# Another issue order on all engines in a windowed-attention, convolution and MLP block

## What is computed

```python
xw = windows(x)                            # 7x7 windows: 64 per image, 49 tokens, 96 channels
xn = layernorm(xw) * ln_g + ln_b
q, k, v = (xn @ qkv_w.T + qkv_b)           # 12 heads of 8
attn = softmax((q * SCALE) @ k.T + bias[REL_IDX])
out = attn @ v
seq = x + window_reverse(out @ proj_w.T + proj_b)
conv = depthwise_conv3x3(seq)              # 9 taps per channel, zero padding
seq2 = batchnorm(conv)                     # mean, variance, gain and shift are given
h = gelu(seq2 @ w1.T + b1)                 # 384 hidden
y = seq2 + (h @ w2.T + b2)
```

## Time and profile before

| | us |
|---|---|
| median of 3 runs | 3174.46 (3173.98 to 3175.64) |
| the profiled execution | 3164.1 |
| its span | 3162.3 |
| TensorE busy | 3029.4 (96%) |
| VectorE busy | 2888.8 (91%) |
| ScalarE busy | 2768.5 (88%) |
| GpSimd busy | 1956.6 (62%) |
| granted TensorE clock, mean | 0.993 of full |

### The profile page before, as it was taken

The page is one execution under the profiler, slowest core; times in us unless marked ns, Lnnn a source line. Parts: engine busy times, 40 slices in busy tenths (PEclk is TensorE's granted clock), DMA queues, the critical chain, the costliest instruction groups (busy, mean ns, idle before and its releaser), DMA issues.

```text
span 3162.3 us, 199772 instructions
## 1 busy us (share of the span) xinstructions
PE 3029.4 (96%) x88076; PEld 2105.9 (67%) x88076; DVE 2888.8 (91%) x4908; ACT 2768.5 (88%) x4867; POOL 1956.6 (62%) x2574
## 2 busy tenths in 40 slices
PE   3899999999999999999999999999999999999997
PEld 2666666666766666666666666666666676666663
DVE  4799999999999999999999999999999999999996
ACT  2799999989989999998989999988989999998986
POOL 2566666666666666666666666666666666666664
PEclk9999999999999999999999999999999999999998
DMA  1233333333333333333333333333333333333331
GB/s 40 86 91 96 91 96 94 92 95 91 97 91 94 95 94 95 96 91 95 91 96 94 94 96 94 92 96 91 95 95 93 96 97 93 95 98 91 95 92 41
DMA packets 269922, 288.31 MB, mean 91 GB/s; under 512 B 55651, under 2 KB 252580, under 8 KB 269062
## 3 DMA queue, kind: packets, MB, share of 16 engines
q1 hardware_dynamic: 236294, 198.40, 22.6%
q0 software_dynamic: 32768, 77.14, 7.0%
HBM read 39.34 MB, written 38.54 MB: 25 GB/s over the span
## 4 chain that ended last, share of the span: by engine, by line
PE 91%; issue 3%; ACT 2%; SPq 1%; DMA 1%; DVE 1%; POOL 0%; POOLq 0%; ACTq 0%; DVEq 0%
PE d_ps L255 21%; PE st_ps L299 12%; PE o_ps L345 11%; PE sm_ps L320 10%; PE b_ps L363 7%; PE b_ps L399 6%; PE a_ps L255 4%; PE b_ps L255 4%; PE a_ps L266 3%; PE a_ps L268 3%; PE a_ps L267 3%; PE d_ps L266 1%; PE d_ps L268 1%; PE b_ps L267 1%; PE d_ps L267 1%
## 5 line engine op out<-in xcount | busy, mean ns | idle before, releaser
L764 DVE SCALAR_TENSOR_TENSOR s<-ximg,cols,s 96x392 f32<-96x392 f32 x1792 | 1137.0, 635 | 30.7 <-POOL s L627 3.2
L738 DVE TENSOR_REDUCE mx<-sm_ps 128x12 f16<-128x588 f32 x1024 | 785.0, 767 | 127.7 <-PE sm_ps L320 125.1
L474 ACT ACTIVATE p<-st_ps 128x588 f32<-128x588 f32 x1024 | 672.4, 657 | 179.2 <-PE st_ps L299 176.1
L637 POOL DMA_DIRECT2D ox<-o_sb x1024 | 582.7, 572 | 30.8 <-ACT o_sb L499 17.2
L320 PEld LDWEIGHTS sm_ps<-k_all,q_all 127*49 127x49 f16 x24576 | 460.6, 104 | 171.5 <-issue 76.0
L255 PE MATMUL d_ps<-g,w_s 128*64 128x392 f32 x3072 | 560.2, 500 | 0.0
L299 PEld LDWEIGHTS st_ps<-q_all,k_all 128*49 128x49 f16 x24576 | 435.5, 103 | 157.2 <-issue 107.8
L610 POOL TENSOR_TENSOR s<-ximg,cols 96x392 f32<-96x392 f32 x256 | 216.0, 844 | 520.5 <-DVE y L801 519.9
L299 PE MATMUL st_ps<-q_all,k_all 128*49 128x49 f16 x24576 | 516.1, 186 | 21.4 <-issue 19.3
L320 PE MATMUL sm_ps<-k_all,q_all 127*49 127x49 f16 x24576 | 508.6, 186 | 25.9 <-issue 15.6
L599 POOL TENSOR_TENSOR xl<-xn,xh 96x392 f16<-96x392 f32 x256 | 258.8, 1011 | 273.6 <-ACT xh L555 256.5
(11 more groups left out here) (122 smaller groups left out, 5959.7 us busy)
## 6 DMA issues: line engine op xcount, KB each, us to landing
ox<-o_sb POOLq DMA_DIRECT2D x1024, 73.5 KB
k_all<-kh SPq DMA_DIRECT2D x512, 75.0 KB
q_all<-qh SPq DMA_DIRECT2D x512, 75.0 KB
x_sb<-in_x SPq DMA_DIRECT2D x256, 147.0 KB, 2.4
out<-y SPq DMA_DIRECT2D x256, 147.0 KB, 2.7
q_all<-ql SPq DMA_DIRECT2D x256, 75.0 KB
k_all<-kl SPq DMA_DIRECT2D x256, 75.0 KB
q_all<-mxt SPq DMA_DIRECT2D x256, 9.4 KB, 2.1
```

The costliest lines, as they stand in the source:

```text
L474: af(p32[:, p, :, :].rearrange("p (b h) n -> p b h n", b=2), st_ps[:, :, 0:HALF].rearrange("p b (h n) -> p b h n", n=TOK), ACT.Exp).then_i ...
L637: nc.gpsimd.dma_start(ox[:, c % 2, x4, :], o_sb[x4::4, c % 2, :, :]).then_inc(o_in[c % 2], 16)
L738: v.tensor_reduce(mx[:, c % 2, 0:HEADS, p].rearrange("p (b h) -> p b h", b=2), sm_ps[:, :, 0:HALF].rearrange("p b (h n) -> p b h n", n=TOK ...
L764: v.scalar_tensor_tensor(acc, image_rows(c, k // 3, k % 3), cw_c[:, k:k + 1], acc, ALU.mult, ALU.add)\
```

## The change

The same operations stand in another order in all five loops; some with another chunk, since they moved past the border between two steps. On TensorE no more than two score or value groups stand side by side. The waits that named the last user of a buffer or an input follow the new order (`p == 3`, `k == 1`, `pv_done[2]`). No operation is added or removed.

```diff
 sync:
             for s in range(STEPS):
-                load(s)
-                first_term(k_all, 0, kh, kh_done, s - 3)
-                term(k_all, 2, kh, kh_done, s - 3)
+                maximum_row(s - 5)
+                first_term(k_all, 2, kh, kh_done, s - 3)
+                term(k_all, 1, kl, kl_done, s - 3)
+                term(q_all, 1, qh, qh_done, s - 3)
+                term(k_all, 0, kh, kh_done, s - 3)
                 term(q_all, 0, qh, qh_done, s - 3)
                 term(q_all, 2, ql, ql_done, s - 3)
-                term(k_all, 1, kl, kl_done, s - 3)
-                term(q_all, 1, qh, qh_done, s - 3)
                 store(s - 11)
-                maximum_row(s - 4)
+                load(s)
 tensor, values_times_p and hidden:
-                elif p == 2:
+                elif p == 3:
                     free(pe, (o_done[0], c), (o_done[1], c-1))
-                if k == 0:
+                if k == 1:
                     wait(pe, sl_done, c)
 tensor:
             for s in range(STEPS):
-                exp_scores(s - 4, 2)
-                max_scores(s - 3, 3)
-                projection(s - 6)
+                values_times_p(s - 4, 0)
+                values_times_p(s - 4, 1)
+                hidden(s - 8, 1)
+                maxima_rows(s - 3)
                 hidden(s - 8, 0)
-                maxima_rows(s - 3)
-                hidden(s - 8, 1)
                 hidden(s - 8, 2)
                 exp_scores(s - 4, 3)
                 max_scores(s - 2, 0)
                 second(s - 8, 0)
                 second(s - 8, 1)
+                max_scores(s - 2, 1)
                 second(s - 8, 2)
+                exp_scores(s - 3, 0)
                 keys(s - 1)
-                max_scores(s - 2, 1)
+                max_scores(s - 2, 2)
                 queries(s - 1)
-                exp_scores(s - 3, 0)
+                exp_scores(s - 3, 1)
                 centred(s)
-                max_scores(s - 2, 2)
-                exp_scores(s - 3, 1)
+                values_times_p(s - 4, 3)
                 values_times_p(s - 4, 2)
-                values_times_p(s - 4, 3)
                 variance(s)
                 values(s - 2)
-                values_times_p(s - 3, 0)
-                values_times_p(s - 3, 1)
+                exp_scores(s - 3, 2)
+                max_scores(s - 2, 3)
+                projection(s - 5)
 scalar, outputs:
-                wait(act, pv_done[1 if half == 0 else 3], c)
+                wait(act, pv_done[1 if half == 0 else 2], c)
 scalar:
             for s in range(STEPS):
+                gelu(s - 8, 0)
                 gelu(s - 8, 2)
                 if real(s - 8):
                     act.preload_act_table_set("natural_log_exp_and_others")
                 exp(s - 4, 3)
+                outputs(s - 4, 0)
+                exp(s - 3, 0)
                 key_high(s - 1)
+                log_sums(s - 5)
                 query_high(s - 1)
-                exp(s - 3, 0)
-                log_sums(s - 5)
+                inverses(s - 5)
                 square(s)
-                inverses(s - 5)
                 exp(s - 3, 1)
-                outputs(s - 4, 1)
                 log_variance(s)
                 root(s)
+                outputs(s - 4, 1)
                 exp(s - 3, 2)
                 if real(s - 7):
                     act.preload_act_table_set("gelu_and_others")
-                gelu(s - 7, 0)
-                outputs(s - 3, 0)
+                gelu(s - 7, 1)
                 input_high(s)
-                gelu(s - 7, 1)
 gpsimd:
             for s in range(STEPS):
-                first_product(s - 6)
-                second_product(s - 6)
-                image_high(s - 7)
-                image_low(s - 7)
                 add_products(s - 6)
                 to_channels(s - 4)
+                second_product(s - 5)
                 input_low(s)
+                first_product(s - 5)
+                image_high(s - 6)
+                image_low(s - 6)
 vector, values_out:
-                wait(dve, pv_done[3], c - 2)
+                wait(dve, pv_done[2], c - 2)
 vector:
             for s in range(STEPS):
-                maxima(s - 2, 2)
+                tap(s - 7, 8)
+                normalise(s - 5)
                 values_out(s - 2)
+                maxima(s - 2, 3)
                 input_normal(s)
-                maxima(s - 2, 3)
                 image_sum(s - 5)
                 tap(s - 6, 2)
                 maxima_out(s - 2)
...
                 tap(s - 6, 4)
                 maxima(s - 1, 0)
                 tap(s - 6, 5)
+                maxima(s - 1, 1)
                 tap(s - 6, 6)
                 block_out(s - 7)
-                maxima(s - 1, 1)
                 key_low(s)
+                maxima(s - 1, 2)
                 query_low(s)
                 tap(s - 6, 7)
-                tap(s - 6, 8)
-                normalise(s - 4)
```

## The result

| | before | after |
|---|---|---|
| median | 3174.22 us (3167.17 to 3175.64) | 3359.31 us (3357.92 to 3363.91) |
| ratio, 95% interval | | 1.058 (1.0563 to 1.0597) |
| profiled span | 3162.3 us | 3358.1 us |
| a mean step (344 matmuls) | 11.92 us | 12.71 us |

The account below looks back on a forecast made before the run. The prediction took TensorE, with its instruction-fetch gaps, to bound the kernel. Its terms, -92 + 36 + 15 + 3 + 23 + 3 = -12 us, gave 3152 us, or 3162 us as median; range 3136 to 3200.

Parts of the forecast that it names:

- Bound: TensorE, busy in 96% of the span, loses 0.36 us a step, 92 us in all, to instruction-fetch gaps.
- 1, bursts removed: TensorE's small groups no longer bunched: most fetches arrive in time, 92 us of gaps gained but for 3 us.
- 2, tile shapes: TensorE changes tile shape seven times a step instead of six: 0.14 us a step, 36 us; clean step 11.70 us.
- 3, ScalarE's path: ScalarE's work between hidden products and first score group ties with TensorE's: new wait, 0.06 us a step, 15 us.
- the 11.8: A clean TensorE step of 11.8 us, instead of 11.70, would show the tile-shape price to be wrong.
- 4, square: ScalarE's square between centring and variance ties with TensorE's work there: 0.01 us a step, 3 us.
- 5, DMAs: Key-term DMAs and the row of maxima for scores have less reserve: 0.09 us a step, 23 us.
- 6, "The rest is covered": Remaining orders, walked with old mean durations, cost nothing; VectorE has 0.9 us a step to spare.
- forecast of a small gain: Bursts gone, new step costs of 0.3 us: 3162 us, own range 3148 to 3168; chance 0.42.
- The slower one (ScalarE's path): ScalarE's path from hidden 1 to first score group sets the step: +36 us, 3198 us; chance 0.15.
- The one on the gaps: TensorE's gaps have a cause any order keeps, such as mean instruction rate: 3251 us; chance 0.08.

Follow-up runs that it names:

- e1: The changed kernel with GpSimd's second_product moved back behind first_product: 3205.47 us, ratio 1.0071 to the kernel before.
- k9: e1 with GpSimd's input_low also waiting for tap 4: 3193.75 us, ratio 1.006 to the kernel before.
- k10: The changed kernel, every order kept, with GpSimd's second_product also waiting for tap 4: 3205.13 us, ratio 1.0094 to the kernel before.
- k6: The kernel before with the 24 matmuls of exp_scores 2, in the dense run, issued twice: 3344.46 us, ratio 1.0535.
- k7: The kernel before with the 24 matmuls of exp_scores 0, in a sparse stretch, issued twice: 3337.34 us, ratio 1.0522.
- k13: The kernel before, every order kept, with GpSimd's input_low also waiting for tap 4: ratio 1.0003.
- e3: The changed kernel with second_product and the wait for it left out: 3206.37 us, ratio 1.0066 to the kernel before.

## Why the prediction was wrong, point by point

- **Bound.** Right: TensorE's gaps in the small groups lie at block borders and cost before 0.33 of the 0.36 us a step that I read out of the earlier trace rows.
- **1, bursts removed.** In after the residue is 0.04 us a step (forecast 0.01). But there VectorE slows the pace; with the collision undone it is 0.10 to 0.15 (e1 0.10, k9 0.14, k10 0.15), mostly in value groups 3 and 2 behind centring. The term was mis-sized by about 0.1 us a step, 26 us: the new order removes a half to two thirds of the gaps. That the mean rate keeps the rest is what k6 and k7 suggest; no run isolates it.
- **2, tile shapes.** Right. The tenth percentiles of all groups add up to 11.70 us in e1 and 11.68 in k9.
- **3, ScalarE's path.** Right in size: in k9 the last second-layer products before `exp_scores` 0 take 0.75 us in the median against 0.69 undisturbed, 0.06 us. An undisturbed step of e1, k9 and k10 is 11.82 us. That is the 11.8 which the prediction had named as a sign against point 2, but the groups' own times keep point 2's 11.70; of the 0.12 above it this wait is half in k9.
- **4, square.** Right: variance waited for it twice (0.3 us) from 200 to 3000 us in after, and as often in e1 and k9.
- **5, DMAs.** Forecast 0.09 us a step. The waits for the row of maxima and for ql add up to 65.9 + 17.4 us in the 231 steps of k9, 0.36 us of idle weight loads a step, of which part is hidden; how much reaches the step isn't separated. I had left the load of 147 KB ahead of the row out of its price; the landing measured 2.8 us, not 2.1.
- **6, "The rest is covered".** This is the step that failed. I walked the new orders with mean durations of the old one, found 0.9 us to spare on VectorE, and even wrote down "four DMA issues, second product, input_low without pause" without asking which VectorE operations run beside these. A tap's duration is not a property of the tap. Its neighbour on GpSimd changed, seven taps grew by 1.28 us a step together, more than the 0.9 to spare, and the step went from 11.92 to 12.71 us instead of 11.87. The 0.9 was too large as well: busy time counts overlapping operations once already, so the earlier trace rows leave 11.92 - 11.28 = 0.64 us. The sign was in the trace of before: the same line took 619 ns in the median and 1377 at most, and of the 41 taps over 900 ns 34 stood beside `input_low` and the other seven beside `second_product`.
- **The rivals.** None had this mechanism. The slower one (ScalarE's path) named a wait that exists but costs 0.06 us. The one on the gaps was right in part: with the collision undone 0.10 to 0.15 of their 0.33 us a step stay.

With the collision undone the forecast of a small gain would still have been off: 1.006 to 1.009 of before. Against e1's 12.07 us a step my 11.87 (clean 11.70, and 0.06, 0.01, 0.09 and 0.01) misses 0.2 us: 0.1 of it are the gaps of point 1, the rest maxima that come late and the DMAs.

## What to carry to other kernels

Before moving an operation on GpSimd, list what VectorE does beside its new place, and look in the trace of before for the spread (min, median, max) of each group, not its mean: a group with a fixed shape whose longest is twice its median asks for a look at what stands beside the long ones (here a GpSimd operation stood beside every tap over 900 ns in before). When two orders are compared by a walk, walk both engines together. A wait removed at one entry of a nearly full engine comes out at the next; read which reader ends last there before paying for the move.

## What the hardware showed beyond what was expected

- **A tap and a GpSimd operation don't run side by side unharmed.** The Trainium skill (SBUF — State Buffer, Who interferes with whom) says that a VectorE instruction with two SBUF inputs contends with a GpSimd instruction that reads SBUF, and that issue order decides which of the two blocks the other. The trace agrees with the first part: `key_low` and `query_low`, with one input in PSUM, took 0.55 us beside `second_product` in before as without it. It agrees with the second where GpSimd had been idle before its operation and the two starts lie well apart. In before tap 4 started at least 0.1 us ahead of such an `input_low` in 211 steps and took at most 0.63 us, while `input_low` took 1.01 us in the median instead of 0.90. In k13 `input_low` started 0.44 us ahead of tap 5 and kept its 0.90 us, and tap 5 took 0.88. It doesn't agree where the operation stands ready behind DMA issues. In after tap 4 started 0.36 us before `second_product` by the records and took 1.64 us, 1.02 more than alone; `second_product` took its usual 0.85 us, and `input_low` behind it 1.24. GpSimd's starts are rough in a profile, so this stays open.
- **Tap 3 was hit as well,** 1.08 us instead of 0.62, though it ended 0.39 us before `second_product` is recorded to start. DMA issues alone beside a tap don't do it: 413 such taps in before took 0.615 us in the mean and 0.624 at most. Why an operation that only stands next in GpSimd's queue already costs is not settled; that removing or delaying it restores tap 3 is shown (e1, e3, k10).
- **Block crossings are not hidden on this kernel.** The Trainium skill (Runtime: NRT & Kernel Launch, Instruction fetch mechanics) calls them mostly hidden. Here they cost 0.33 us a step in before, and single issue waits reached 1.1 us in before and 2.2 in k6.
- **A small DMA behind a large one lands later:** 9.4 KB after 2.8 us with the 147 KB load issued just before it, 2.4 with the load just after.
